# A hybrid layer on one core: no barrier between batches, and another order of the first projections and value tiles

## The chip, the cores and the metric

One Trainium2 chip, one of its cores. The metric is the device time of one execution in microseconds (us). The core's engines work side by side, each through its own list of instructions in order, and meet at semaphores: TensorE (PE: matrix products and transposes, into PSUM), VectorE (DVE), ScalarE (ACT), GpSimd (POOL), and SyncE (SP), which issues most DMA transfers. PSUM has eight banks of 128 x 512 float32.

## The reference

Four batches of 1024 tokens, 512 wide, go through four sublayers. Each has a layer norm in front and is added to its input:

```python
x = x + attention(layernorm(x))   # 16 heads of 32, Wqkv 512 x 1536; softmax over keys, Wo
x = x + experts(layernorm(x))     # 8 experts of rank 16, the best 2 by softmax gates
x = x + ssm(layernorm(x))         # 32 heads, state 64, depthwise convolution, gated, W_out
x = x + experts(layernorm(x))     # the same experts again
```

In the attention, `kqv = x @ Wqkv + bqkv` is cut in three; the scores are of k against q under a triangular mask, a softmax over the keys weighs v. Nothing of one batch enters another.

## The kernel before, in words

A loop on every engine runs over the batches (b, 0 to 3). A float32 product at full precision is made as three products of float32r halves ("hi" and "lo"; `three`, L713 to L717): ScalarE rounds a tile to its hi part, VectorE or GpSimd subtracts for the lo part.

**Layer norm.** Token tiles t = 0 to 7 of 128 tokens. VectorE takes statistics (`tile_stats`, L1345), GpSimd the inverse root in two halves of four tiles (`inverse_roots`, L1747), VectorE normalises a tile into `xh` (`center`, L1371), TensorE transposes it in four pieces (`turn`, L725), ScalarE copies the hi part into `uh` (L1126), VectorE makes the lo part `ul` (`lo`, L1362). `by_tile` puts a product of tile t-1 behind the transposes of tile t. `add_tiles` adds a stage's result to X and, where another layer norm follows, takes the statistics of tile t-1 between additions and normalises the first two tiles at t = 5.

**Opening of the attention.** A value tile is 12 matmuls, one token tile times the value weights wv (`values`), evicted by VectorE with its bias (`value`, L1471). A projection of a head group (4 heads) is four pieces: ch 0 and 1 are the first operand for tokens 0 to 511 and 512 to 1023, ch 2 and 3 the second; 12 matmuls each (`project`), evicted by ScalarE (hi, L1179) and VectorE (lo, L1488). Then DMAs (`stack`, L461) bring the parts of each pair of heads into rows QS and KS. A first pass of scores (`scores_a`, L830, 16 steps t16) is only for each row's maximum, which VectorE takes (L1496); the maxima are turned (L838), copied and sent by DMA into QS as one more row. The second pass (`scores_b`, L850) makes scores with the maximum subtracted; ScalarE takes exponentials (L1202), TensorE weighs the values (L867, L869). While one pair of heads is weighed, the first pass of the next pair and the next group's projection run between its steps.

Before, value tiles 0 to 3 lie among the transposes, then come tiles 4 to 7's transposes without products, the four projection pieces of group 0, and value tiles 4 and 5, 6, and 7 ahead of score steps 0, 4 and 8 (`EARLY`, `BETWEEN`).

**Group weights.** The weights of a head group go to `win` in two steps: a cast on ScalarE (`group_hi`, L1149) and a subtraction on GpSimd (`group_lo`, L1751, one instruction). The value weights take four casts (L1165) and four subtractions. On GpSimd, the second half of the inverse roots, the copies of the values (VG, L1773), a memset and eight additions of the bias bo to X (L1785) stand in the opening; then comes group_lo of the next group.

**Batch boundary.** The last expert stage ends with additions to X. `barrier` then holds TensorE, ScalarE, VectorE and GpSimd until all have come; SyncE stores the tiles of X as they are done, and loads the next batch's tokens into X, a tile behind its store (L534). The weights of the value product and of head group 0 are loaded beside the expert stage, after the row product of the ssm stage.

## Time and profile before

| | |
|---|---|
| median of 3 runs | 3359.28 us (3359.22 to 3366.12) |
| the profiled execution's own time | 3359.53 us |
| its span in the profile | 3357.7 us |
| TensorE busy | 3056.9 us, 91% of the span |
| VectorE busy | 2206.4 us, 66% |
| ScalarE busy | 1095.1 us, 33% |
| GpSimd busy | 753.4 us, 22% |
| mean granted clock of TensorE | 0.94 |

The span is from the first to the last instruction. "Granted clock" (PEclk) is the share of full speed that the chip gives TensorE: it is 1.0 (2.4 GHz) or 0.5 (1.2 GHz), and a stretch between is a mixture. The program's start lasts until about 113 us, then come four batches of some 812 us. A row of the timeline has its start, its length, the engine, the kernel's line, the operation, its output <- its inputs and how many instructions it sums up; in brackets the engine's idle time before it and what ended it. Matmuls overlap, so that the length of one is more than the step from one to the next.

### The profile page before, as it was taken

The page shows a single profiled execution, that of the slowest core. Times are in us where ns is not written, and L with a number is a line of the kernel's source. Part 1 is how long each engine was busy: PE and PEld are TensorE (multiplying, and loading weights), DVE is VectorE, ACT ScalarE, POOL GpSimd, SP SyncE. Part 2 cuts the span into 40 slices and gives each one's busy share as a digit, 9 for nine tenths or more (in the row PEclk, how much of TensorE's full clock was granted, in tenths as well). Part 3 has the DMA queues.
Part 4 walks back from the last instruction along what each step waited for, and adds up shares of the span by engine and source line. Part 5 has one row for each costly group of instructions (what it writes and reads, how often), then busy time and mean ns, then how long its engine had stood idle before and what let it go on. Part 6 is the DMA issues. An engine that isn't in the chain of part 4 may idle for free.

```text
span 3357.7 us, 59614 instructions
## 1 busy us (share of the span) xinstructions
PE 3056.9 (91%) x20772; PEld 2086.8 (62%) x20772; DVE 2206.4 (66%) x2961; ACT 1095.1 (33%) x1728; POOL 753.4 (22%) x1065
## 2 busy tenths in 40 slices
PE   3599999999879998999978999999997999999998
PEld 3445457777555446777755444777775454577775
DVE  1356667777646667777764666777764566677776
ACT  1123314444113333344312332343421233143441
POOL 3121102333031111233311110133321211013331
PEclk6789999999979999999988999999998899999999
DMA  7422102111131211111121220111112121021111
GB/s 228 149 50 63 45 13 64 51 48 44 49 82 44 63 26 46 50 48 44 35 83 45 63 63 20 51 44 51 42 43 83 45 69 45 13 63 50 48 42 51
DMA packets 160037, 189.47 MB, mean 56 GB/s; under 512 B 43834, under 2 KB 103866, under 8 KB 158074
## 3 DMA queue, kind: packets, MB, share of 16 engines
q1 hardware_dynamic: 155998, 173.74, 18.8%
q0 software_dynamic: 2720, 10.49, 0.8%
q10 hardware_dynamic: 1152, 3.15, 0.4%
q8 instruction: 89, 1.46, 0.2%
q14 instruction: 78, 0.64, 0.1%
HBM read 104.90 MB, written 23.36 MB: 38 GB/s over the span
## 4 chain that ended last, share of the span: by engine, by line
PE 77%; DVE 9%; issue 4%; DMA 4%; SPq 3%; ACT 2%; POOL 1%; DVEq 0%; POOLq 0%; ACTq 0%
PE ps L715 13%; PE ps L717 12%; PE ps L716 12%; PE ps L867 7%; PE ps L830 5%; PE ps L850 5%; PE ps L1026 4%; PE ps L912 3%; PE ps L1012 2%; DVE mneg L1496 2%; PE ps L760 2%; PE ps L1072 2%; DVE LM L1590 2%; PE ps L1035 2%; PE ps L725 1%
## 5 line engine op out<-in xcount | busy, mean ns | idle before, releaser
L715 PE MATMUL ps<-uh,win 128*128 128x512 f32 x1536 | 631.1, 411 | 10.5 <-DVE ul L1362 5.9
L717 PE MATMUL ps<-uh,win 128*128 128x512 f32 x1536 | 606.0, 395 | 0.0
L716 PE MATMUL ps<-ul,win 128*128 128x512 f32 x1536 | 602.9, 393 | 0.0
L1496 DVE TENSOR_REDUCE mneg<-ps 128x1 f32<-128x128 f32 (+7 forms) x512 | 360.5, 751 | 164.6 <-PE ps L833 160.9
L1202 ACT ACTIVATE PR<-ps 128x1024 f32<-128x1024 f32 (+3 forms) x384 | 310.6, 810 | 430.1 <-PE ps L853 292.8
L867 PE MATMUL ps<-PR,VG 128*32 128x512 f32 (+3 forms) x1536 | 346.3, 528 | 10.8 <-DVE OS L1502 8.3
L715 PEld LDWEIGHTS ps<-uh,win 128*128 128x128 f32 x1536 | 291.5, 190 | 103.7 <-issue 36.5
L869 PE MATMUL ps<-PR,ones 128*32 128x512 f32 (+3 forms) x1536 | 346.3, 528 | 0.0
L717 PEld LDWEIGHTS ps<-uh,win 128*128 128x128 f32 x1536 | 290.6, 189 | 65.9
L1614 DVE TENSOR_TENSOR LM<-ps,LM 128x512 f32<-128x512 f32 x256 | 170.2, 686 | 241.5 <-PE ps L1026 197.1
L716 PEld LDWEIGHTS ps<-ul,win 128*128 128x128 f32 x1536 | 291.9, 190 | 55.1
L1838 POOL TENSOR_SCALAR_AFFINE_SELECT LM<-LM 128x512 f32<-128x512 f32 x256 | 209.0, 827 | 490.8 <-ACT LM L1281 490.8
L850 PE MATMUL ps<-QS,KS 97*128 97x512 f32 (+3 forms) x768 | 274.6, 424 | 15.5 <-DMA QS<-mrow 8.9
L830 PE MATMUL ps<-KS,QS 96*128 96x512 f32 (+3 forms) x768 | 247.2, 422 | 26.6 <-DMA KS<-EV 16.4
L1801 POOL TENSOR_TENSOR OT<-OS,rec 64x512 f32 (+1 forms) x64 | 82.5, 1288 | 838.5 <-DVE rec L1509 838.5
L1602 DVE SCALAR_TENSOR_TENSOR Ct<-ps,cpt,Ct 128x1023 f32<-128x1023 f32 (+2 forms) x192 | 245.5, 1279 | 16.6 <-ACT Ct L1271 12.1
L1602 DVE SCALAR_TENSOR_TENSOR Bt<-ps,cpt,Bt 128x1023 f32<-128x1023 f32 (+2 forms) x192 | 243.5, 1268 | 0.3
L850 PEld LDWEIGHTS ps<-QS,KS 97*128 97x128 f32 x768 | 148.1, 207 | 137.8 <-issue 90.8
L830 PEld LDWEIGHTS ps<-KS,QS 96*128 96x128 f32 x768 | 139.4, 211 | 137.4 <-DVE mneg L1496 70.1
L1126 ACT CAST uh<-ps 128x512 fp32r<-128x512 f32 x128 | 74.0, 588 | 453.0 <-PE ps L725 453.0
L1509 DVE RECIPROCAL rec<-OS 64x256 f32<-64x256 f32 (+1 forms) x96 | 214.6, 2261 | 2.1
L1281 ACT ACTIVATE LM<-ps 128x512 f32<-128x512 f32 x256 | 147.6, 602 | 124.3 <-PE ps L1012 124.1
(218 smaller groups left out, 5149.6 us busy)
## 6 DMA issues: line engine op xcount, KB each, us to landing
raw<-in_t SPq DMA_DIRECT2D x128, 256.0 KB, 2.8
QS<-EV SPq DMA_DIRECT2D x192, 128.0 KB, 2.4
KS<-EV SPq DMA_DIRECT2D x168, 128.0 KB, 2.4
X<-in_L_attn_b_W_in_dram SPq DMA_DIRECT2D x10, 1024.0 KB, 8.0
in_t<-tiles POOLq DMA_DIRECT2D x10, 1024.0 KB, 9.0
win_raw<-in_L_attn_a_Wqkv_dram SPq DMA_DIRECT2D x34, 256.0 KB, 3.5
X<-in_L_attn_a_x_dram SPq DMA_DIRECT2D x32, 256.0 KB, 3.9
win_raw<-in_t SPq DMA_DIRECT2D x32, 256.0 KB, 2.7
```

The lines of the kernel that those rows point to most:

```text
L715: pe.matmul(dst, hi_l, hi_r, start=first, stop=False)
L716: pe.matmul(dst, hi_l, lo_r, start=False, stop=False)
L717: return pe.matmul(dst, lo_l, hi_r, start=False, stop=last)
L830: i = pe.matmul(ps[:, b0 + c // HB, 0:m], QS[slot][0:STACK, hh, t * P:(t + 1) * P], KS[slot][0:STACK, hh, c:c + m], start=True, stop=not diag)
L850: i = pe.matmul(ps[:, SCORE_BANK[u] + hh, 0:n], KS[slot][:, hh, s * P:(s + 1) * P], QS[slot][:, hh, t0:t0 + n], start=True, stop=not diag)
L867: pe.matmul(ps[o:o + HS, 6, at:at + n], VG[:, s, h:h + HS], PR[:, u % 2, hh, 0:n], start=(s == 0), stop=last)
L869: i = pe.matmul(ps[r:r + HS, 6, at:at + n], ones[:, 0:HS], PR[:, u % 2, hh, 0:n], start=(s == 0), stop=last)
L1202: act.activation(PR[:, u % 2, :, 0:n], ps[:, SCORE_BANK[u]:SCORE_BANK[u] + 2, 0:n], ACT.Exp, scale=SCALE).then_inc(ex.sem, 1)
L1496: dve.tensor_reduce(mneg[:, hh, t:t + 1], wide(b0)[:, 0:(t + 1) * P], AX.X, ALU.max, negate=True).then_inc(a_max.sem, 1)
L1509: i = dve.reciprocal(rec[hf * 64:(hf + 1) * 64, cols], OS[(1 - hf) * 64:(2 - hf) * 64, cols])
L1602: dve.scalar_tensor_tensor(dst[:, par, k:L], wide(2 * w)[:, 0:L - k], cpt[:, par, w, at:at + 1], dst[:, par, k:L], ALU.mult, ALU.add).then ...
L1838: pool.affine_select(out=v, in_=v, compare_op=ALU.is_ge, fill=0.0, base=0, pattern=[[0, 4], [1, P]], channel_multiplier=-1).then_inc(sel_p ...
```

## The change

1. The barrier is gone. The tokens of the next batch are loaded into a tile XN of their own (in memory that OT and other tiles use at other times), right behind the row product of the ssm stage, ahead of the last expert stage's stores. Statistics and the first two normalised tiles of the next batch are taken in `add_tiles` of the last expert stage. The bias addition on GpSimd becomes X = XN + bob.
2. The value weights of the next batch are loaded at the last pair of the ssm stage, cast and subtracted at that stage's end (`value_hi`, `value_lo`). Group 0's cast (`group_hi`) follows the first exponentials of the last expert stage on ScalarE; its subtraction and the first half of the inverse roots follow on GpSimd. For batch 0 all this stands ahead of the loop.
3. The opening has another order: transposes 0 and 1, value tile 0, transposes 2, value tile 1, transposes 3 to 5, the projection piece ch 0, transposes 6, ch 2, transposes 7, value tile 2, ch 1, ch 3, value tiles 3 and 4; tiles 5 and 6 in quarters (`value_part`) between score steps, tile 7 half ahead of the turned maxima and half behind them.
4. The row tiles of the second slot lie over wv now, so SyncE waits for the last value tile before it fills them. In the last batch the prepared "next" batch is batch 3 again, and nothing uses it.

```diff
-EARLY = HALF
-BETWEEN = {0: (4, 5), 4: (6,), 8: (7,)}
+FIRST_OF = (0, 2, 1, 3)
+BETWEEN = {3: (5, 0), 5: (5, 1), 6: (5, 2), 7: (5, 3), 11: (6, 0), 13: (6, 1), 14: (6, 2), 15: (6, 3)}
+def value_bank(t):
+    return 2 + t % 2 if t < 4 else t
+def first_at(ch):
+    return FIRST_OF.index(ch) + 1
...
-        def barrier(eng, b):
-            eng.sem_inc(s_tick, 1)
-            eng.drain().then_inc(s_bar, 1)
-            eng.wait_ge(s_bar, b * 5 + 10)
-            eng.sem_inc(s_tick, 1)
...
+                XN = sb("XN", [P, TT, D], at=c2)
...
 SyncE
-                    sp.wait_ge(s_out[t], b * 16 + 16)
-                    sp.dma_start(X[:, t, :], x[bass.ds(b, 1), t * P:(t + 1) * P, :].rearrange("a p d -> p (a d)")).then_inc(s_x[t], 16)
+                    sp.dma_start(XN[:, t, :], x[bass.ds(b, 1), t * P:(t + 1) * P, :].rearrange("a p d -> p (a d)")).then_inc(s_x[t], 16)
...
+                            v_pe.wait(sp, b, TT)
                             st_pe.wait(sp, b * 8 + g * 2, 0)
                             stack(sp, 1)
...
+                                if last and q == 3:
+                                    xp_pool.wait(sp, b * PAIRS + j, 1)
+                                    value_weights()
                                 save_y(j, q)
...
                     w_pe.wait(sp, b * 2 + 1, TT)
-                first_weights()
-                sp.sem_inc(s_tick, 1)
-                sp.drain().then_inc(s_bar, 1)
+                    group_weights(0)
+                    load_tokens(b if end else b + 1)
...
 TensorE
+                turn(b * 4, 0)
+                turn(b * 4, 1)
+                values(0)
+                turn(b * 4, 2)
+                values(1)
+                for t in range(3, 6):
+                    turn(b * 4, t)
+                ln_lo.wait(pe, b * 4, 4)
+                project(0, 0, True)
+                turn(b * 4, 6)
+                project(0, 2, True)
+                turn(b * 4, 7)
+                values(2)
                 ln_lo.wait(pe, b * 4, TT)
-                for ch in range(4):
-                    project(0, ch, True)
+                project(0, 1, True)
+                project(0, 3, True)
+                values(3)
+                values(4)
+                v_done.wait(pe, b, 4)
                 for t16 in range(16):
-                    late_values(t16)
+                    if t16 in BETWEEN:
+                        value_part(*BETWEEN[t16])
                     scores_a(b * 8, 0, b * 4, t16)
+                for k in range(2):
+                    value_part(7, k)
                 turn_maxima(b * 8)
+                for k in range(2, KT):
+                    value_part(7, k)
                 pe.wait_ge(s_kone, b * 2 + 1)
-                v_done.wait(pe, b, TT)
                 scores_b(b * 8, 0, b * 4, 0)
+                v_done.wait(pe, b, TT)
...
 ScalarE
-                experts(b * 4 + 3, b * 2 + 1)
-                barrier(act, b)
+                value_hi(b + 1)
+                experts(b * 4 + 3, b * 2 + 1, lambda: group_hi(b * 4 + 4))
...
 VectorE
+                def behind(t):
+                    if t < 2:
+                        value(t)
+                    elif t == 4:
+                        project_lo(0, 0, True)
+                    elif t == 5:
+                        project_lo(0, 2, True)
+                    elif t == 6:
+                        value(2)
+                by_tile(b * 4, behind, lambda: loaded(b, TT - 1), XN)
...
-                experts(b * 4 + 3, b * 2 + 1, None, lambda: w_add.wait(dve, b * 2 + 1, TT))
-                barrier(dve, b)
+                experts(b * 4 + 3, b * 2 + 1, b * 4 + 4, lambda: w_add.wait(dve, b * 2 + 1, TT), XN, lambda t: loaded(b + 1, t))
...
 GpSimd
+            value_lo(0)
+            inverse_roots(0, (0,))
+            group_lo(0)
+            with pool.Fori(0, NB) as b:
+                inverse_roots(b * 4, (1,))
...
-                    i = pool.tensor_tensor(X[:, t, :], X[:, t, :], bob[:, :], ALU.add)
+                    pool.wait_ge(s_out[t], b * 16 + 16)
+                    pool.sem_inc(s_tick, 1)
+                    i = pool.tensor_tensor(X[:, t, :], XN[:, t, :], bob[:, :], ALU.add)
...
+                value_lo(b + 1)
                 inverse_roots(b * 4 + 3)
-                barrier(pool, b)
+                group_lo(b * 4 + 4)
+                inverse_roots(b * 4 + 4, (0,))
```

TensorE behind the last product of a value tile among the transposes (xh the normalised tile, win the group's weights), before:

```order
L717 MATMUL ps<-wv,ul 128x512
L95 REGISTER_ALU
L725 MATMUL ps<-ident,xh 128x128 x4
L95 REGISTER_ALU
L725 MATMUL ps<-ident,xh 128x128 x4
L95 REGISTER_ALU
L725 MATMUL ps<-ident,xh 128x128 x4
L95 REGISTER_ALU
L715 MATMUL ps<-uh,win 128x512
```

and in the changed kernel:

```order
L725 MATMUL ps<-wv,ul 128x512
L103 REGISTER_ALU
L733 MATMUL ps<-ident,xh 128x128 x4
L103 REGISTER_ALU
L733 MATMUL ps<-ident,xh 128x128 x4
L103 REGISTER_ALU
L733 MATMUL ps<-ident,xh 128x128 x4
L103 REGISTER_ALU
L723 MATMUL ps<-uh,win 128x512
```

The rows read alike, but before they are tiles 5, 6 and 7 behind value tile 3, and now tiles 3, 4 and 5 behind value tile 1, so that the first projection piece has two more tiles' transposes still to come.

TensorE between the first pass of scores (its mask's matmul is the first row) and the second, with the transpose of the maxima mneg, before:

```order
L833 MATMUL ps<-mask_ts,identb 128x128
L95 REGISTER_ALU
L838 MATMUL ps<-ident,mneg 16x128
L880 ISA
L95 REGISTER_ALU
L844 ISA
L95 REGISTER_ALU
L850 MATMUL ps<-QS,KS 128x512
```

and in the changed kernel, up to the waits ahead of the second pass:

```order
L725 MATMUL ps<-wv,ul 128x512
L103 REGISTER_ALU
L846 MATMUL ps<-ident,mneg 16x128
L723 MATMUL ps<-wv,uh 128x512
L724 MATMUL ps<-wv,uh 128x512
L725 MATMUL ps<-wv,ul 128x512
L723 MATMUL ps<-wv,uh 128x512
L724 MATMUL ps<-wv,uh 128x512
L725 MATMUL ps<-wv,ul 128x512
L909 ISA
L852 ISA
```

Half of value tile 7 stands ahead of the transpose of the maxima, and the other half behind it.

GpSimd at the end of a batch, behind the last selection in the ssm stage, before:

```order
L1838 AFFINE_SELECT LM<-LM 128x512
L95 ISA
L1747 TENSOR_TENSOR rstd<-veps,halfs 128x4
L95 REGISTER_ALU
L1747 TENSOR_TENSOR rstd<-veps,halfs 128x4
L346 ISA
```

and in the changed kernel, from the last two subtractions for wv on:

```order
L1796 TENSOR_TENSOR wv<-wv_raw,wv 128x512
L103 REGISTER_ALU
L1796 TENSOR_TENSOR wv<-wv_raw,wv 128x512
L103 ISA
L1792 TENSOR_TENSOR rstd<-veps,halfs 128x4
L103 REGISTER_ALU
L1792 TENSOR_TENSOR rstd<-veps,halfs 128x4
L103 REGISTER_ALU
L1796 TENSOR_TENSOR win<-win_raw,win 128x2x512
L103 ISA
L1792 TENSOR_TENSOR rstd<-veps,halfs 128x4
```

In place of the barrier's signal stand the next batch's group_lo and the first half of its inverse roots, and ahead of the stage's own roots the value weights.

## Rows read from the trace of the kernel before

**Rows 1.** The page, part 1: busy us, share of the span, instructions.

```profile
PE 3056.9 (91%) x20772; PEld 2086.8 (62%) x20772; DVE 2206.4 (66%) x2961; ACT 1095.1 (33%) x1728; POOL 753.4 (22%) x1065
```

**Rows 2.** Waits: engine, line, for whom; us in total, times, longest.

```profile
PE ps L725 <- DVE xh L1371: 68.9, 12, 18.7
```

**Rows 3.** Timeline, TensorE: first transposes of batches 1, 2 and 3.

```profile
932.14 1.97 PE L725 MATMUL ps<-ident,xh 128*128 128x128 f32 x8 [14.96 <-DVE xh L1371]
...
1744.88 1.54 PE L725 MATMUL ps<-ident,xh 128*128 128x128 f32 x6 [15.29 <-DVE xh L1371]
...
2557.45 1.97 PE L725 MATMUL ps<-ident,xh 128*128 128x128 f32 x8 [15.18 <-DVE xh L1371]
```

**Rows 4.** Timeline, batch 1's opening: TensorE, and VectorE's last eight maxima.

```profile
954.70 0.79 PE L715 MATMUL ps<-uh,win 128*128 128x512 f32 x1 [1.48 <-DVE ul L1362]
...
972.79 0.22 PE L830 MATMUL ps<-KS,QS 96*128 96x128 f32 x1
...
983.51 5.54 DVE L1496 TENSOR_REDUCE mneg<-ps 128x1 f32<-128x128 f32 x8
...
989.11 0.38 PE L838 MATMUL ps<-ident,mneg 128*16 128x128 f32 x1 [1.32 <-DVE mneg L1496]
991.71 0.79 PE L850 MATMUL ps<-QS,KS 97*128 97x512 f32 x1 [2.22 <-DMA QS<-mrow]
```

**Rows 5.** Timeline, TensorE: the opening of batch 0, first and last.

```profile
122.78 1.54 PE L725 MATMUL ps<-ident,xh 128*128 128x128 f32 x6 [18.66 <-DVE xh L1371]
...
179.46 0.79 PE L850 MATMUL ps<-QS,KS 97*128 97x512 f32 x1 [2.22 <-DMA QS<-mrow]
```

**Rows 6.** Windows: stretch, its us, busy by engine (instructions), PEclk, DMA share, GB/s.

```profile
957.00:970.00 13.00, 13.00 (x57) 10.64 (x56) 3.01 (x4) 2.75 (x4) 0.00 (x0) 0.97 0.27 62
...
897.00:907.00 10.00, 6.32 (x15) 2.22 (x13) 8.72 (x38) 1.26 (x7) 0.00 (x0) 0.66 0.00 1
490.30:493.70 3.40, 3.40 (x19) 3.40 (x18) 2.84 (x10) 0.23 (x1) 2.31 (x2) 0.50 0.01 2
991.70:1009.10 17.40, 16.90 (x76) 7.94 (x76) 4.44 (x7) 5.16 (x7) 7.57 (x6) 0.50 0.51 122
```

**Rows 7.** Timeline, TensorE: first expert stage of batch 0 into the next norm.

```profile
486.89 0.49 PE L761 MATMUL ps<-bu,w3T 24*128 24x512 f32 x1
487.31 1.09 PE L725 MATMUL ps<-ident,xh 128*128 128x128 f32 x8
489.92 0.39 PE L715 MATMUL ps<-waw,uh 128*128 128x256 f32 x1 [1.51 <-DVE ul L1362]
```

**Rows 8.** Timeline: GpSimd and VectorE together; the gates' exponentials; TensorE behind the gates.

```profile
492.49 2.70 POOL L1751 TENSOR_TENSOR win<-win_raw,win 128x512 fp32r<-128x512 f32 x2
492.73 1.31 DVE L1371 TENSOR_SCALAR xh<-X,mv,rstd 128x512 f32<-128x512 f32 x1
...
895.87 0.23 ACT L1133 ACTIVATE gex<-ge_ 128x32 f32<-128x32 f32 x1 [1.07 <-DVE ge_ L1416]
...
900.86 0.47 PE L753 MATMUL ps<-ident,hg 128*128 128x128 f32 x1 [3.60 <-DVE hg L1436]
```

**Rows 9.** Timeline, GpSimd: from the value copies to the next group's subtraction.

```profile
983.76 1.16 POOL L1773 COPY VG<-V 128x512 f32<-128x512 f32 x2 [33.78 <-DVE V L1471]
...
987.06 9.85 POOL L1785 TENSOR_TENSOR X<-X,bob 128x512 f32<-128x512 f32 x8 [0.18 <-POOL KS L1781]
997.33 2.36 POOL L1751 TENSOR_TENSOR win<-win_raw,win 128x1024 fp32r<-128x1024 f32 x1 [0.42 <-POOL X L1785]
```

**Rows 10.** Timeline, ScalarE: first and seventh exponentials of two pairs of heads.

```profile
993.33 1.30 ACT L1202 ACTIVATE PR<-ps 128x1024 f32<-128x1024 f32 x2 [3.55 <-PE ps L853]
...
1014.24 0.59 ACT L1202 ACTIVATE PR<-ps 128x512 f32<-128x512 f32 x1
...
313.25 1.02 ACT L1202 ACTIVATE PR<-ps 128x1024 f32<-128x1024 f32 x1 [0.83 <-PE ps L853]
...
328.23 0.59 ACT L1202 ACTIVATE PR<-ps 128x512 f32<-128x512 f32 x1
```

More of the change, by code:

```diff
@@ L726, in turn, with by_tile @@
                 i.then_inc(ln_tp.sem, 1)
-            def by_tile(n, product, tiles=TT):
+            def by_tile(n, product):
                 for t in range(TT + 1):
@@ L1120, in _, with turn @@
             first_barrier(act)
-            def turn(n):
-                for t in range(TT):
+            def turn(n, tiles=range(TT)):
+                for t in tiles:
                     ln_tp.wait(act, n, t + 1)
@@ L1176, in project_hi @@
                                 act.wait_ge(s_stack[i][hh], (b * 4 + g) * 96)
-                    pj.wait(act, b * 4 + g, ch + 1)
+                    pj.wait(act, b * 4 + g, first_at(ch) if first else ch + 1)
                     act.sem_inc(s_tick, 1)
@@ L1395, in add_tiles, with experts @@
                     dve.tensor_tensor(X[:, t, :], ps[:, bank + t % 4, :], X[:, t, :], ALU.add).then_inc(added.sem, 1)
[L1396 to L1398 removed]
+                    if t >= 1:
+                        if loaded is None:
+                            added.wait(dve, n, t)
+                        else:
+                            loaded(t - 1)
+                        tile_stats(stats_of, t - 1, src)
                         if t == HALF + 1:
[L1400 to L1402 removed]
+                            first_tiles(stats_of, src)
+            def experts(n, f, stats_of, last_added, src=X, loaded=None):
                 ch = Chain(dve, s_gates, 26, f)
@@ L1456, in pair_lo, with loaded @@
                                   ALU.subtract).then_inc(bcw_lo.sem, 1)
+            def loaded(b, t):
+                dve.wait_ge(s_x[t], b * 16 + 16)
+                dve.sem_inc(s_tick, 1)
+            for t in range(TT - 1):
+                loaded(0, t)
+                tile_stats(0, t, XN)
+                if t == HALF:
+                    first_tiles(0, XN)
             with dve.Fori(0, NB) as b:
@@ L1486, in project_lo @@
                     cols = slice(c * HB, (c + 1) * HB)
-                    pj_hi.wait(dve, b * 4 + g, ch + 1)
+                    pj_hi.wait(dve, b * 4 + g, first_at(ch) if first else ch + 1)
                     dve.scalar_tensor_tensor(EV[w][1][:, cols], ps[:, 4 + ch if first else 7, :],
@@ L1490, in project_lo @@
                                              EV[w][0][:, cols].bitcast(F32), ALU.add, ALU.subtract).then_inc(pj_lo.sem, 1)
+                def behind(t):
[8 more added lines that the diff above has]
+                by_tile(b * 4, behind, lambda: loaded(b, TT - 1), XN)
+                project_lo(0, 1, True)
+                project_lo(0, 3, True)
+                for t in range(3, 5):
+                    value(t)
                 def maximum(p, t16):
@@ L1740, in until, with inverse_roots @@
                 pool.sem_inc(s_tick, 1)
-            def inverse_roots(n):
-                for h in range(2):
+            def inverse_roots(n, halves=(0, 1)):
+                for h in halves:
                     until(ln_var, n, h + 1)
```

371 lines of the change are left out of this document (183 added, 188 removed).

## The prediction

> **What bounds the kernel now.** I read the page first: TensorE is busy for 91% of the span [rows 1], so only two things can move the end by much: time in which TensorE stands still, and time in which it runs at the lower clock. The waits come next: TensorE's costliest wait is for the first transposes of a layer norm, 68.9 us in 12 waits [rows 2]. The timeline says where: the three largest inside the loop stand at the batch boundaries, 14.96, 15.29 and 15.18 us [rows 3]. All engines meet at the barrier there, the tokens are loaded, their statistics taken, and only then does TensorE start. Last I read the opening of the attention stage, piece by piece, in a batch behind a boundary [rows 4] and in the first [rows 5], and the granted clock of a few stretches [rows 6].
>
> The opening runs from the first transpose (932.14) to the first score matmul of the second pass (991.71): 59.6 us [rows 3, 4]. At the full clock a matmul of this kind takes 13.0/57 = 0.228 us [rows 6], so a value tile or a projection (12 matmuls) is 2.74 us. The 12 of them are 32.8 us; the rest is scores, transposes, standing still and low clock. In the first batch it takes 179.46 - 122.78 = 56.7 us [rows 5].
>
> **The change part by part.**
>
> *A. Boundary.* The barrier goes; tokens land in a tile of their own, XN, issued before the second expert stage, and VectorE takes their statistics and first two normalised tiles between its last additions. This trace has a stage built so already, the first expert stage into the next layer norm: the last expert matmul starts at 486.89, the transposes at 487.31, with no idle time between them [rows 7]. I take that for all three boundaries: 14.96 + 15.29 + 15.18 = **45.4 us off**. Were the tokens late, part of the stand would stay, so the bounds are 0 and 45.4; but the load is issued ahead of the whole expert stage and read behind its end, so I take all of it. What is late next is the chain from transpose to the first product, 489.92 - 487.31 = 2.6 us [rows 7].
>
> *B. Opening.* From the first transpose on: 2.6 us to the first product [rows 7]; then, before the first score, five value tiles and four projections, 108 x 0.228 = 24.6; six more groups of transposes at 0.4 us (half of some 0.8 for eight in [rows 7]) 2.4; a stretch at the low clock like the 3.4 us behind the same kind of start [rows 6], which costs half of it, 1.7; one gap while transposes 3 to 5 follow each other without a product between them. Before, tiles 5 to 7 stood so, and their last wait alone was 1.48 [rows 4]; I take 1.6, and 0.9 for a one-in-two chance that the clock falls there again. Sum 33.8. Then the scores: VectorE's maxima for one half take 5.54 us [rows 4], two halves 11.1, and and I estimate one value copy at 0.7, the start at 0.3 and waits for free banks at 1.7: 13.8 until the last maximum. TensorE's own work there, two value tiles in quarters (5.5) and scores (an estimated 6), is less and lies beside it; half of the last value tile follows while the last maxima run. Then 0.5 to the transpose of the maxima and its 991.71 - 989.11 = 2.6 us to the second pass [rows 4], which now hides the other half tile. Total 33.8 + 13.8 + 0.5 + 2.6 = 50.7 against 59.6: 8.9 each in three batches, **26.6 off**. Bounds: nothing in the opening runs faster than work plus the two chains (about 46), and 59.6 is what it takes now.
>
> *C. First batch.* There GpSimd's subtraction for the first head group (group_lo) now comes right behind the first half of the inverse roots, that is beside VectorE's first two normalisations. The nearest row of such a meeting: GpSimd started at 492.49, VectorE's normalisation, begun at 492.73, ended at 494.04, just behind the end of GpSimd's first instruction (2.70/2 = 1.35 us, to 493.84) [rows 8]. Group_lo is one instruction of 2.36 us [rows 9], so the bounds are 0 and 2.4 and I take 2.4 lost; a little low clock that the old opening had there too gives 1.2 less than in B. 50.7 + 2.4 - 1.2 = 51.9 against 56.7: **4.8 off**.
>
> *D. The first pair of heads.* Behind the opening TensorE ran at the low clock for the whole of 991.7 to 1009.1, busy for 16.9 of 17.4 us [rows 6]. From the first exponential to the seventh it took 1014.24 - 993.33 = 20.9 us; the same piece of a later group took 328.23 - 313.25 = 15.0 [rows 10]. So a full clock would be worth 5.9 us a batch. It can't be had whole: GpSimd is queued behind the last value tile with two copies, a memset, eight additions of 9.85 us and group_lo, 999.69 - 983.76 = 15.9 us [rows 9], and these now start some 0.3 us behind the first score matmul of the second pass, where they started 8 us ahead of it. The next projection needs group_lo; with its 2.74 us and 1.1 more to the seventh exponential that one can't come before 20.0 us, against 22.5 now (1014.24 - 991.71). So 0 to 2.5 a batch; I take 1.3, **5.2 off**.
>
> *E. Expert stage.* ScalarE casts the next batch's group weights right behind the first exponentials (895.87 [rows 8]), so GpSimd's group_lo of 2.36 us starts near 897.3, in the middle of VectorE's chain of small gate operations, which ends what TensorE waits for: it stood still for 3.60 us until 900.86 [rows 8]. If VectorE is held as it was at 492.73, the chain is late by what is left of 2.36. Bounds 0 and 2.4; I take 2.4, since the chain is a row of short operations with gaps into which the long one can fall: 4 x 2.4 = **9.6 lost**. The longer stand also keeps the clock low for longer than the few us of 897 to 907 (0.66 granted [rows 6]): 0 to 4 a batch, taken as 1, **4 lost**. The Trainium skill (SBUF — State Buffer, "SBUF: two separate sides") says that a VectorE operation with two inputs in SBUF is blocked for the whole of a GpSimd operation that reads SBUF; most gate operations are of that kind. The row at 492.73 is of another kind and agrees as far as it goes; without that rule I would have put E at half.
>
> *F. Costed at nothing.* The value weights are loaded, cast and subtracted behind the last pair's mixing, while VectorE's last gate and TensorE's row product run: ScalarE and GpSimd have nothing else there. If GpSimd's four subtractions (4 x 9.85/8 = 4.9 us by [rows 9]) came 2 us late they would meet VectorE's last gate, up to 5 us. The additions of the bias now read XN; their wait for the stores of the last batch was over long before. SyncE's wait for the last value tile ahead of the second slot's rows is over before it gets there; behind it stand only those row copies. The reload of tokens after the last batch is hidden by the expert stage.
>
> **Sum.** 45.4 + 26.6 + 4.8 + 5.2 - 9.6 - 4 = 68.4 us off. The profiled execution took 3359.5 us (span 3357.7), 0.2 above the median of 3359.28, so no correction: 3359.5 - 68.4 = **3291 us**.
>
> **Rivals.**
> *1. The clock holds and the gates aren't held up.* E goes (13.6), the 0.9 and 1.7 of B mostly go (some 8 in all): 3269. For: 957 to 970 ran at 0.97 [rows 6]. Against: each start behind a stand of 1.5 us or more in these rows has a low stretch behind it. 0.20.
> *2. Low clock for long.* In one of the two places (behind the gates, behind transposes 3 to 5) the clock stays low for some 20 us as in 991.7 to 1009.1 [rows 6], not 3.4: (20 - 3.4)/2 = 8.3 a batch, 3291 + 33 = 3324. For: the stand behind the gates grows from 3.6 to 6 us. 0.16.
> *3. The stretch doesn't do what it says:* the overlap works, but the reordered opening is paced by VectorE and ScalarE, whose in-order queues now carry a projection's halves between tiles (ul, EV, V one behind the other), and gives nothing, or the boundary keeps a third of its stand for a late load: 3291 + 31 = 3322 at the middle, 3307 to 3337. Against: each tile has 2.74 us of products beside it, and VectorE has an estimated 2 us of work a tile. 0.12.
> *4. Slower than before.* The low clock takes the opening and the pairs behind it: at half speed every 2 us of busy time lose 1. It decides from 68.4/4 = 17 us lost a batch, that is 34 us more of TensorE's time at the low level than now; with 50 us more a batch it is 25 x 4 = 100 lost, 3391. For: 17.4 us in one piece stand there now. Against: the change takes stands away everywhere but behind the gates. 0.04.
> The forecast has 0.48, within 3277 to 3307.
>
> **Range and chances.** 3291 is the likeliest. The range takes in rival 1 and rivals 2 and 3 to their middles: 3265 to 3324; left out are rival 4, the far half of 3, and the tails. A measurement of this kernel tells 0.2% (7 us) from no change. Faster is all but rival 4 and a remnant for mishaps: 0.95; same 0.01; slower 0.04.
>
> **What would show it.** A: no wait of TensorE near 15 us at the three boundaries, transposes within 0.5 us of the last expert matmul. B: first transpose to first score of the second pass in 49 to 53 us; if over 56, the reordering failed. D: first to seventh exponential under 19 us, and a wait of the next projection for GpSimd's subtraction. E: a gate operation of VectorE that takes over 2 us, and TensorE's wait behind the gates at 6 us instead of 3.6. I am wrong if the first-to-last times of an expert stage don't grow (then E), or if a stretch of 20 us at the low clock stands in a new place (rival 2).

## The result, and the profile after

The changed kernel takes **3305.8 us** (median of 4 runs, 3297.8 to 3327.7) against 3359.6 beside it: ratio **0.984, 95% interval 0.981 to 0.988**. A second comparison gave 0.985 (0.981 to 0.989). The forecast of 3291 us (3265 to 3324) holds: faster, by 54 us where 68 were worked out. The profiled execution took 3303.4 us, so I read 56 us out of its trace. Ratios and ranges, here and below, are of fast runs; left out as slow are one run of the second comparison (10760.6 us) and two of experiment 5 (3397.6 and 3398.6).

| | before | after |
|---|---|---|
| profiled execution / span, us | 3359.5 / 3357.7 | 3303.4 / 3301.8 |
| mean granted clock | 0.94 | 0.952 |
| TensorE busy, us | [rows 1] | 3038.8 |

The page, part 1:

```profile
PE 3038.8 (92%) x20772; PEld 2076.8 (63%) x20772; DVE 2220.3 (67%) x2975; ACT 1095.8 (33%) x1733; POOL 759.9 (23%) x1071
```

Waits (engine, line, for whom: us in total, times, longest), against [rows 2]:

```profile
PE ps L761 <- DVE hg L1475: 37.5, 8, 5.8
PE ps L733 <- DVE xh L1407: 25.5, 9, 20.7
PE ps L838 <- DMA KS<-EV: 21.6, 19, 1.4
PE ps L723 <- POOL win L1796: 8.9, 6, 3.3
```

The wait for the first transposes fell from 68.9 to 25.5 us; what is left is mostly the 20.7 of the very first, before batch 0. The wait for the gated tiles (hg) has grown from 28.9 us to 37.5, and that for GpSimd's subtraction (win) from 4.0 to 8.9.

**A, boundary.** TensorE at the first boundary, and VectorE beside it, against [rows 3]:

```profile
914.80 0.50 PE L769 MATMUL ps<-bu,w3T 24*128 24x512 f32 x1
916.81 1.16 PE L733 MATMUL ps<-ident,xh 128*128 128x128 f32 x8 [1.51 <-issue]
```

```profile
916.50 0.68 DVE L1381 BATCH_NORM_STATS2 stats<-XN 128x6 f32<-128x512 f32 x1
918.67 0.69 DVE L1398 TENSOR_TENSOR ul<-ps,uh 128x512 fp32r<-128x512 f32 x1 [1.50 <-ACT uh L1155]
```

From the last expert matmul to the next transposes it takes 2.01, 2.02 and 2.47 us, before 15.45, 15.79 and 15.67 (starts, the idle time of [rows 3] and the last matmul's own time): 40.4 us off. The stand that is left is put down to "issue": TensorE waited for no other engine.

**B, C, opening.** First scores and second pass of batch 1, and a window behind the boundary (stretch, its us, busy by engine, PEclk, DMA share, GB/s), against [rows 4, 6]:

```profile
952.12 0.33 PE L838 MATMUL ps<-KS,QS 96*128 96x128 f32 x1 [0.84 <-DMA KS<-EV]
...
969.09 0.49 PE L858 MATMUL ps<-QS,KS 97*128 97x512 f32 x1 [0.82 <-DMA QS<-mrow]
```

```profile
917.70:924.50 6.80, 5.27 (x14) 3.95 (x13) 2.89 (x9) 0.89 (x2) 2.94 (x2) 0.50 0.56 184
```

969.09 - 916.81 = 52.3 us, in the other two batches 51.7 and 51.8, before 59.6, 59.3 and 59.2: 22.2 off. In batch 0 the opening is 51.7 against 56.7, 4.9 off. The meeting foreseen in C took place, ahead of the first transposes; the row of the same two normalisations before, and three rows now:

```profile
122.18 1.00 DVE L1371 TENSOR_SCALAR xh<-X,mv,rstd 128x512 f32<-128x512 f32 x2 [0.61 <-POOL rstd L1747]
```

```profile
119.85 2.33 POOL L1796 TENSOR_TENSOR win<-win_raw,win 128x1024 fp32r<-128x1024 f32 x1
119.90 3.03 DVE L1407 TENSOR_SCALAR xh<-XN,mv,rstd 128x512 f32<-128x512 f32 x2 [0.59 <-POOL rstd L1792]
122.52 1.12 PE L733 MATMUL ps<-ident,xh 128*128 128x128 f32 x4 [20.66 <-DVE xh L1407]
```

**D, first pair of heads.** First and seventh exponential, and the next projection on TensorE, against [rows 9, 10]:

```profile
970.05 1.30 ACT L1238 ACTIVATE PR<-ps 128x1024 f32<-128x1024 f32 x2 [2.89 <-PE ps L861]
...
990.76 0.59 ACT L1238 ACTIVATE PR<-ps 128x512 f32<-128x512 f32 x1
```

```profile
985.36 0.50 PE L723 MATMUL ps<-uh,win 128*128 128x512 f32 x1 [3.28 <-POOL win L1796]
```

The window from the first exponential until the subtraction is done, and the one from there to the seventh exponential:

```profile
970.00:985.30 15.30, 10.12 (x79) 4.94 (x77) 6.24 (x9) 5.00 (x7) 14.38 (x11) 1.00 0.57 133
985.30:990.80 5.50, 5.44 (x25) 4.09 (x25) 0.00 (x0) 0.62 (x2) 0.00 (x1) 0.69 0.00 0
```

From the second pass to the seventh exponential it is 21.2 to 21.7 us, before 22.4 to 22.5: 4.2 off in four batches.

**E, second expert stage.** GpSimd and VectorE, then TensorE behind the gates, the stage's first transposes ahead of them, and the window behind, against [rows 6, 8]:

```profile
873.92 1.04 PE L733 MATMUL ps<-ident,xh 128*128 128x128 f32 x8
...
891.05 2.34 POOL L1796 TENSOR_TENSOR win<-win_raw,win 128x1024 fp32r<-128x1024 f32 x1 [12.39 <-ACT win L1180]
891.09 2.58 DVE L1462 SCALAR_TENSOR_TENSOR gq<-gt,before 128x256 f32<-128x256 f32 x1
893.71 0.42 DVE L1463 SCALAR_TENSOR_TENSOR gq<-gt,gq 128x256 f32<-128x256 f32 x1
...
896.86 0.48 PE L761 MATMUL ps<-ident,hg 128*128 128x128 f32 x1 [5.76 <-DVE hg L1475]
```

```profile
893.80:907.50 13.70, 10.56 (x20) 3.98 (x21) 10.24 (x39) 1.67 (x9) 0.00 (x0) 0.50 0.11 39
```

The gate operation gq takes 2.58 us, beside GpSimd's subtraction of 2.34, where the like one behind it takes 0.42. TensorE stands for 5.76 instead of 3.60 us, and the clock is at its lower level for all of 893.8 to 907.5 (before, 897 to 907 had a mean of 0.66). From the first transposes to the last matmul, 914.80 - 873.92 = 40.9 us, in the others 39.7, 41.0 and 40.9; before 36.3 to 36.6: 16.4 lost. Of these 8.6 lie in the first half of the stage, up to the transposes of the gated tiles, with 2.15 in every batch (22.95 us against 20.80); 7.8 lie in the second half, and that part varies: 17.9, 16.7, 18.1 and 17.9 us in this trace, 14.6, 14.8, 19.5 and 16.6 in the second trace of the same kernel, before 15.5 to 15.8.

Sum: 40.4 + 22.2 + 4.9 + 4.2 - 16.4 = 55.3 of the spans' 55.9. The stages that the sum leaves out moved too, and nearly cancel: the attention behind the first pair is 4.7 us shorter in sum, the ssm stage 2.7 longer and the first expert stage 1.0.

### The profile page after: what moved, and what is told of

It is laid out like the page before. It is cut to its first block, busy times and chain, and to the rows that moved or that the text cites. A ratio compares the mean times of both kernels' runs of the same rounds, so it can differ in the third digit from the quotient of the medians.

```text
span 3301.8 us, 59660 instructions
## 1 busy us (share of the span) xinstructions
PE 3038.8 (92%) x20772; PEld 2076.8 (63%) x20772; DVE 2220.3 (67%) x2975; ACT 1095.8 (33%) x1733; POOL 759.9 (23%) x1071
## 4 chain that ended last, share of the span: by engine, by line
PE 76%; DVE 9%; issue 4%; DMA 4%; SPq 3%; ACT 2%; POOL 1%; ACTq 0%; DVEq 0%; POOLq 0%
PE ps L723 13%; PE ps L725 12%; PE ps L724 12%; PE ps L875 7%; PE ps L838 5%; PE ps L858 5%; PE ps L1056 4%; PE ps L942 3%; PE ps L1042 2%; PE ps L1102 2%; DVE LM L1636 2%; PE ps L1065 2%; PE ps L768 2%; DMA KS<-EV 1%; DVE mneg L1543 1%
## 5 line engine op out<-in xcount | busy, mean ns | idle before, releaser
L875 PE MATMUL ps<-PR,VG 128*32 128x512 f32 (+3 forms) x1536 | 338.3, 517 | 12.4 <-DVE OS L1549 8.3
L877 PE MATMUL ps<-PR,ones 128*32 128x512 f32 (+3 forms) x1536 | 338.3, 517 | 0.0
L858 PE MATMUL ps<-QS,KS 97*128 97x512 f32 (+3 forms) x768 | 266.4, 414 | 9.9 <-ACT PR L1238 6.6
L838 PE MATMUL ps<-KS,QS 96*128 96x512 f32 (+3 forms) x768 | 239.4, 411 | 29.1 <-DMA KS<-EV 21.6
L1648 DVE SCALAR_TENSOR_TENSOR Ct<-ps,cpt,Ct 128x1023 f32<-128x1023 f32 (+2 forms) x192 | 245.6, 1279 | 16.6 <-ACT Ct L1307 12.0
```

What stands on the lines that cost most here:

```text
L838: i = pe.matmul(ps[:, b0 + c // HB, 0:m], QS[slot][0:STACK, hh, t * P:(t + 1) * P], KS[slot][0:STACK, hh, c:c + m], start=True, stop=not diag)
L858: i = pe.matmul(ps[:, SCORE_BANK[u] + hh, 0:n], KS[slot][:, hh, s * P:(s + 1) * P], QS[slot][:, hh, t0:t0 + n], start=True, stop=not diag)
L875: pe.matmul(ps[o:o + HS, 6, at:at + n], VG[:, s, h:h + HS], PR[:, u % 2, hh, 0:n], start=(s == 0), stop=last)
L877: i = pe.matmul(ps[r:r + HS, 6, at:at + n], ones[:, 0:HS], PR[:, u % 2, hh, 0:n], start=(s == 0), stop=last)
L1648: dve.scalar_tensor_tensor(dst[:, par, k:L], wide(2 * w)[:, 0:L - k], cpt[:, par, w, at:at + 1], dst[:, par, k:L], ALU.mult, ALU.add).then ...
```

## The experiments

Each ratio is to the kernel before, timed beside the variant. The changed kernel and the late cast were timed beside each other once, in the second comparison.

**1. The late cast** (timed three times, the second and third beside other variants).

```diff
                 exponentials(0)
-                if meanwhile is not None:
-                    meanwhile()
@@ (loop over t, behind the copies of a tile)
+                    if t == 4 and meanwhile is not None:
+                        meanwhile()
```

> The changed kernel, but ScalarE casts the next batch's group weights behind the fifth pair of copies of the last expert stage, not behind the first exponentials; GpSimd's subtraction follows it there, behind VectorE's gate operations. Theory (GpSimd's subtraction of 2.34 us holds VectorE's gate operation for as long as it runs): no gate operation over 0.5 us, TensorE's longest wait behind the gates back from 5.8 to about 3.6 us, second expert stage from its first transposes to its last matmul back from 40.6 to 36.6-37.5 us in each batch, 13 to 16 us off the changed kernel's 3303.4: 3288 to 3291. Rival 1 (the stage is longer because VectorE now does the next batch's statistics between its additions, or because the clock falls there anyway): it stays at 40 us or more, the time within 3 us of 3303. Rival 2 (the block only moves, to VectorE's additions or the first normalised tiles): the gates are free, but the last additions or the next first transposes come up to 2.3 us later, and of the 13 us under 6 are left.

Measured: 3275.2 us, ratio **0.976** (0.973 to 0.979).

```profile
PE ps L761 <- DVE hg L1475: 28.8, 8, 3.6
```

```profile
886.45 0.42 DVE L1462 SCALAR_TENSOR_TENSOR gq<-gt,before 128x256 f32<-128x256 f32 x1
...
890.07 0.47 PE L761 MATMUL ps<-ident,hg 128*128 128x128 f32 x1 [3.61 <-DVE hg L1475]
```

The operation is back at 0.42 us, the stage at 36.3, 35.8, 35.4 and 36.4 us: 18.6 us less than with the early cast. So rival 1 falls. The boundaries got 1.7 us longer in sum, but only 0.2 in the second pair of traces, so rival 2 isn't shown. The spans differ by 29.9 us. The other 13 lie in stages that the edit doesn't touch: the attention stages behind the first pair are 9.3 us shorter, at a mean granted clock of 0.962 instead of 0.952 over the whole run.

> The changed kernel itself once more, beside its variants on one chip. Both theories expect the 0.984 of the first comparison (3306), within 3295 to 3320, since the granted clock differs from run to run.

> The kernel of the late cast once more, beside the changed kernel on the same chip. Its first comparison gave 3275 where 16 us off 3304 were expected from the stage alone. Theory A (the stand behind the gates also set how long the clock stays low behind it, in the expert stage and in the stages that follow): the distance to the changed kernel stays 25 us or more, with a mean granted clock higher by about 0.01. Theory B (the surplus was chance of one profiled run and four timings): 14 to 20 us off the changed kernel.

Measured on one chip: 0.985 (0.981 to 0.989) for the changed kernel, 0.976 (0.973 to 0.980) for the late cast. That is 28 us apart, near theory A, but by these intervals uncertain by some 18 us, so that the 14 to 20 of theory B aren't excluded; and the granted clock, averaged over the runs, is higher by 0.004 (0.951 and 0.956), not by theory A's 0.01. A third time the late cast gave 0.979 (0.975 to 0.983), as expected there:

> The late cast once more, as the yardstick for the next kernel on the same chip: 0.976 of the kernel before, within 0.973 to 0.980.

What the traces show in every pair is the hold: the first half of the stage takes 22.95 us with the early cast and 20.80 with the late one, 8.6 us in four batches. The rest goes with the clock. The whole stage took 162.4 and 157.3 us (four batches) in the two traces of the changed kernel, and 143.8, 151.0 and 158.5 in the three of the late cast; two batches of the third took 43.0 us, each with 20 us at the low clock behind the usual stand of 3.6. The times put the edit at some 24 to 28 us, give or take 10 to 18. That this is more than the hold of 8.6 is likely by the times; by which path a shorter stand would give a higher clock these runs don't show, and no single trace carries it (in the second comparison the two profiled runs were at 0.955 and 0.957).

**2. Memsets in place of the subtraction** (the low part of the next head group's weights is zero in batches 1 to 3).

```diff
-                group_lo(b * 4 + 4)
+                until(qkw_hi, b * 4 + 4, 1)
+                pool.memset(win[:, 0, 0, 1].bitcast(F32), 0.0)
+                pool.memset(win[:, 0, 1, 1].bitcast(F32), 0.0).then_inc(qkw_lo.sem, 1)
```

> The changed kernel, but in the last expert stage of each batch GpSimd fills the low part of the next head group's weights with zeros in two memsets, at the place where it subtracted (so this low part is left out of the computation in batches 1 to 3; GpSimd writes as many elements to the same tile, and reads none). Theory (it is the read of two tiles in SBUF by GpSimd that holds VectorE's operation with two inputs in SBUF): the gate operation gq takes 0.43 us beside the memsets, the stage 36.6-37.5 us. Rival (any work of GpSimd at that time holds VectorE, or the write alone): gq takes as long as the memsets that it meets, 1 us or more, the stage 39 us or more.

```profile
885.30 0.52 POOL L1921 MEMSET win<- 128x512 f32 x1 [12.39 <-ACT win L1180]
885.36 0.42 DVE L1462 SCALAR_TENSOR_TENSOR gq<-gt,before 128x256 f32<-128x256 f32 x1
885.77 0.52 POOL L1922 MEMSET win<- 128x512 f32 x1
888.97 0.48 PE L761 MATMUL ps<-ident,hg 128*128 128x128 f32 x1 [3.60 <-DVE hg L1475]
```

One run, 3280.0 us. The gate operation ran its 0.42 us wholly inside the first memset, at the same place. Theory right: what held it was that GpSimd read SBUF. That a memset is shorter isn't the reason: experiment 3's subtractions are as short (3.70/8 = 0.46 us) and still hold it. This is the rule that the prediction took from the Trainium skill (SBUF — State Buffer, "SBUF: two separate sides"), both of its halves now shown: a GpSimd operation that reads held gq, one that only writes didn't. Three of the four stages took 36.3 to 36.7 us; that of batch 0 took 43.0, with 20 us at the low clock behind the usual 3.6 us stand. So the clock behind the same stand varies.

**3. The subtraction in eight.**

```diff
-                group_lo(b * 4 + 4)
+                until(qkw_hi, b * 4 + 4, 1)
+                for w in range(2):
+                    for k in range(KT):
+                        i = lo_in_place(win[:, 0, w, 0, k], win[:, 0, w, 1, k], win_raw[:, 0, w, 1, k])
+                i.then_inc(qkw_lo.sem, 1)
```

> The changed kernel with the early cast, but in the last expert stage GpSimd's subtraction of 128x1024 goes as eight of 128x128. Theory (VectorE is held for as long as the one GpSimd instruction that it meets runs, so short ones hold it for a part each, and each further gate operation with two inputs in SBUF for the next part): gq takes under 1 us, but the whole chain of gate operations is late by 1 us or more, the stage's first half ends 0.8 to 2.2 us later than in the kernel before. Rival (VectorE goes first between two short instructions and is no longer held): from the stage's first transposes to the first transposes of gated tiles 21.0 us or less.

```profile
889.09 3.70 POOL L1796 TENSOR_TENSOR win<-win_raw,win 128x128 fp32r<-128x128 f32 x8 [12.41 <-ACT win L1180]
889.13 0.70 DVE L1462 SCALAR_TENSOR_TENSOR gq<-gt,before 128x256 f32<-128x256 f32 x1
889.86 0.56 DVE L1463 SCALAR_TENSOR_TENSOR gq<-gt,gq 128x256 f32<-128x256 f32 x1
```

gq took 0.70, the first half of the stage 21.98 us in every batch: 1.18 late, where one piece made it 2.15 and none 0 (20.80). Theory right. Small pieces halve the hold (one run, 3286.1 us), but putting the subtraction elsewhere takes it away.

**4. The boundary alone**: the changed kernel with the old opening.

```diff
-FIRST_OF = (0, 2, 1, 3)
-BETWEEN = {3: (5, 0), 5: (5, 1), 6: (5, 2), 7: (5, 3), 11: (6, 0), ...}
+FIRST_OF = (0, 1, 2, 3)
+BETWEEN = {0: (4, 5), 4: (6,), 8: (7,)}
...
+                for t in range(TT + 1):
+                    if t < TT:
+                        turn(b * 4, t)
+                    if t >= 1:
+                        ln_lo.wait(pe, b * 4, t)
+                        if t <= HALF:
+                            for k in range(KT):
+                                value_part(t - 1, k)
+                for ch in range(4):
+                    project(0, ch, True)
```

> The changed kernel with the old order in the opening of the attention stage (four value tiles among the transposes, four projections, four value tiles between the scores), but no barrier and the next batch prepared early. Theory (the parts add up): boundaries 40 us shorter than before, second expert stages 16 us longer in sum, opening 59 us as before, first batch and first pair unchanged: 3359.5 - 40 + 16 = 3335, within 3330 to 3341. Rival (the two parts need each other: the early preparation puts the stand into the opening unless the transposes are followed by products at once): openings of batches 1 to 3 above 61 us, time 3342 or more. Rival 2 (the loss in the expert stage comes with the new opening, not with the overlap): expert stage at 36.6, time about 3319.

Measured: 3328.8 us, ratio 0.991 (0.988 to 0.994), 1 us under the expected range. Boundaries 2.2 to 2.8 us, second expert stages 37.6 to 39.7, openings 57.2, 57.3, 56.7 and 56.4. In batches 1 to 3 the openings are 2 to 3 us shorter than before without any new order, which no theory had. The trace has the reason: up to the first score TensorE was at the low clock for 12.1, 11.7 and 11.5 us before, with 8.1 to 8.7 of them right behind the stand of 15 us; behind a stand of 2 to 3 us it is 6.8, 3.4 and 3.4. The overlap alone is worth some 30 us, and the new order on top of it 0.991 - 0.984 = 0.7%, 23 us.

**5. The new order alone**: the kernel before with the new opening, barrier and loading as they were. The functions are those of the change; only VectorE's list differs, since the last two statistics are still taken among the tiles:

```diff
+                def behind(t):
+                    if t < 2:
+                        loaded_stats(t + 6)
+                        value(t)
```

> The kernel before with only the new order in the opening (the first head group projected by halves among the transposes, value tiles 5 to 7 in parts between and behind the scores); barrier and loading at the start of a batch as before. Theory (the parts add up): opening 52 instead of 59.6 us in batches 1 to 3 and 52 instead of 56.7 in batch 0, first pair about 1 us shorter each, boundaries 15.5 us and expert stages 36.6 us as before: 22 + 5 + 4 = 31 us off, 3328, within 3322 to 3334. Rival (the new order depends on the statistics being done ahead; with two of VectorE's statistics among the tiles and GpSimd's subtraction behind both inverse roots the products wait for them): opening 56 us or more, time 3342 or more.

Measured: 3360.9 us (median of eight runs), ratio **0.998** (0.995 to 1.002), scattered from 3330 to 3375. Theory wrong, the rival nearer, though two openings are under its 56 us. The opening of batch 0 (GpSimd, VectorE, TensorE):

```profile
132.63 1.98 DVE L1406 TENSOR_SCALAR xh<-X,mv,rstd 128x512 f32<-128x512 f32 x1
134.48 1.87 POOL L1809 MEMSET KS<- 1x2048 f32 x1 [0.16 <-POOL win L1793]
...
134.66 1.12 PE L734 MATMUL ps<-ident,xh 128*128 128x128 f32 x4 [1.83 <-DVE xh L1406]
135.13 1.50 DVE L1406 TENSOR_SCALAR xh<-X,mv,rstd 128x512 f32<-128x512 f32 x1
```

Without the early preparation the second half of the inverse roots and the subtraction (131.81 to 134.33) come among the tiles. Normalisations that take 0.55 us take 1.98 and 1.50, and TensorE waits 1.29 and 1.83 us for them. The openings take 56.5, 54.7, 56.3 and 53.3 us: 13.9 off instead of the 27 with both parts. And the attention stages behind the first pair are 18.3 us longer than before; the granted clock of this run is 0.938. Whether the new order brings this on is open: the same stages, 1013 us in sum here, lie between 981 and 1009 in the other traces, and this profiled run is 8 us slower than the median. The parts don't add up: experiment 4's 30 us and this one's 6 (uncertain by 11) make 36 of the 54. In the openings the trace says why: the new order pays fully only with the statistics and the subtraction out of its way.

**6. The bias later** (on top of the late cast). GpSimd's batch loop's first group is unrolled, and the eight additions stand behind its subtraction:

```diff
-                for t in range(TT):
-                    ...
-                    i = pool.tensor_tensor(X[:, t, :], XN[:, t, :], bob[:, :], ALU.add)
...
                                 until(qkw_lo, b * 4 + g + 1, 1)
+                                if stage == 0:
+                                    for t in range(TT):
+                                        ...
+                                        i = pool.tensor_tensor(X[:, t, :], XN[:, t, :], bob[:, :], ALU.add)
```

> The late cast, and GpSimd's eight additions of the bias moved behind its subtraction for the second head group. Theory (this order is what makes TensorE wait 3.28 us for the subtraction in the first pair of heads): this wait is gone, from the first to the seventh exponential 17 to 18.5 instead of 20.5 us, 8 to 12 us off the kernel with the late cast alone in four batches. Rival (the low clock behind the opening sets this piece, and only fills the time that the wait took, or the earlier work brings the low clock back): the piece stays above 20 us, under 3 us off.

Measured: 0.978 (0.974 to 0.982), the late cast alone on that chip 0.976: no gain seen, though the theory's 8 to 12 us lie within these intervals. The granted clock, averaged over the runs, is 0.951 against 0.956. Two windows, of batches 1 and 3:

```profile
983.00:1004.00 21.00, 20.19 (x108) 10.69 (x106) 6.94 (x10) 6.27 (x9) 14.36 (x11) 0.67 0.41 96
2566.00:2584.00 18.00, 16.04 (x120) 9.37 (x123) 7.96 (x14) 6.26 (x10) 14.82 (x12) 1.00 0.47 115
```

TensorE's wait of 3.28 us is gone in all batches, yet the seven exponentials take 23.6, 20.4, 20.5 and 15.7 us: only where the clock was full (1.00) did the piece come near its 15 us. In the others it was at the lower level for 20.5, 13.7 and 13.7 us; the window of 983 to 1004, behind the opening of batch 1, has TensorE busy for 20.19 of 21 us at 0.67. So the rival holds in three of four batches. With the next edit on top, two of four batches took 15.4 and 15.6 us; in the traces with the additions at their old place none took under 19.

**7. The branch early**, on top of 6 and then without it.

```diff
+            turn(0, 0)
+            turn(0, 1)
             with pe.Fori(0, NB) as b:
-                turn(b * 4, 0)
-                turn(b * 4, 1)
                 ...
                 experts(b * 4 + 3, b * 2 + 1)
+                turn(b * 4 + 4, 0)
+                turn(b * 4 + 4, 1)
@@ vector, before the loop with b = 0 and at its end with b + 1
+                lo(b * 4, 0)
+                loaded(b, TT - 1)
+                tile_stats(b * 4, TT - 1, XN)
```

> The kernel before this one, and the batch loop's end moved: TensorE issues the next batch's first two tiles of transposes, and VectorE the first low half and the last statistics, ahead of the branch back to the loop's start instead of behind it. Theory (the 2.0 to 2.9 us between the last expert matmul and the next transposes are TensorE's branch of 3.5 us, and the first product waits for VectorE's branch too): transposes within 0.6 us of the last matmul, from the last expert matmul to the first product 3.0 to 3.6 instead of 4.7 us, 3 to 5 us off in three boundaries. Rival (the branch only moves to the next place where an engine is waited for): the last matmul to the third tile of transposes takes as long as now, within 1 us of the kernel before this one.

> The late cast, and the batch loop's end moved behind the next batch's first transposes, with GpSimd's bias additions back at their old place. Theory (the branch is hidden and what the kernel with all three edits lost came from the bias additions, behind which the clock fell): 3 to 5 us off the late cast alone, mean granted clock as there. Rival (each stand of TensorE that goes is paid for by a longer stretch at the low clock, wherever the stand was): granted clock lower by 0.004 or more, time the same as the late cast's or up to 12 us more.

```profile
913.29 0.49 PE L769 MATMUL ps<-bu,w3T 24*128 24x512 f32 x1
913.72 1.09 PE L733 MATMUL ps<-ident,xh 128*128 128x128 f32 x8
917.62 0.49 PE L723 MATMUL ps<-wv,uh 128*128 128x512 f32 x1 [2.81 <-issue]
```

These rows are of the first kernel. The transposes follow the last matmul by 0.42 us, as first predicted for the change, so the 2 us were the branch. But it now stands ahead of the first product: last matmul to first product 4.3, 3.8 and 4.2 us here, 4.7 to 5.1 in the changed kernel and 4.9 to 5.5 with the late cast. To the third tile of transposes it is 8.5 and 8.1 us in two boundaries (10.0 to 10.3 with the late cast) and 10.5 in the third, at the low clock. So the first kernel's theory is right on the transposes and missed its 3.0 to 3.6 us for the product; its rival's "within 1 us" holds in one boundary of three. The times show no gain: 0.982 (0.978 to 0.986) with experiment 6's edit, 0.981 (0.979 to 0.984) without, the late cast on that second chip 0.979 (0.975 to 0.983). An edit of 3 to 5 us is finer than these intervals. The second kernel's rival has the time right; its clock, in the mean 0.951 against the late cast's 0.954, fell by 0.003 where 0.004 or more was asked, within the scatter of single runs (0.947 to 0.960).

**Nothing was clearly faster than the changed kernel with the late cast**: 0.976, 0.976 and 0.979, some 2.3% under the kernel before.

## Why the prediction was right, and where it was 13 us off

| term | predicted | measured in the trace |
|---|---|---|
| A boundary | 45.4 off | 40.4 off |
| B opening, batches 1 to 3 | 26.6 off | 22.2 off |
| C first batch | 4.8 off | 4.9 off, by luck |
| D first pair | 5.2 off | 4.2 off |
| E expert stage | 13.6 lost | 16.4 lost |

**A** was mis-sized by its model. The first expert stage runs into the next norm in straight code; the second ends a batch, and behind it TensorE branches back to the loop's start. The trace's record of this branch lasts 3.5 us (913.13 to 916.63), partly beside matmuls already issued. Before, it ran from 918.25 to 922.12, while TensorE stood for VectorE until 932.14 anyway: it was hidden. Experiment 7 shows that the 2 us are the branch's. I had asked whether the load or the transposes' chain would be late; nothing was late but the instructions themselves.

**B** is off by 1.2 us a batch, and by 0.7 because I took batch 1's 59.6 for all three. The clock is low for 6.8 us behind the boundary's stand, not 3.4; that is 1.7 us by the prediction's own price. TensorE waits 0.84 us for the copies into KS ahead of the first score, for which I had no term. Against that the clock didn't fall in the gap among the transposes (0.9). The second pass starts 14.5 + 2.5 us behind the first score, as worked out (14.3 + 2.6). What the 8.9 a batch didn't name is that a part of them belongs to A: the stand of 15 us left the clock low for over 8 us of the old opening, and experiment 4 has 2 to 3 us of the gain without any new order.

**C** came out by luck. The hold took place: the two normalisations beside GpSimd's subtraction took 3.03 us instead of 1.00. But it lies ahead of the first transposes, which come 2.6 us behind the start of the normalisations instead of 0.6. These 2.0 us are outside the interval that was summed, and the earlier statistics covered them (first transposes at 122.52, before 122.78). Inside it batch 0 took 51.7 us like the other batches, and not 1.2 more than they. The prediction had added those 1.2 to a B that was 1.2 too short.

**D** held in its mechanism, and one term of it was mis-sized. TensorE waited 3.28 us for GpSimd. The subtraction ended 16.2 us behind the second pass, as worked out (0.3 + 15.9); from there to the seventh exponential it took 5.0 to 5.5 us, where 2.74 + 1.1 stood. The windows show why: the clock was full until the wait, and fell behind it, so that the 12 matmuls of the projection took 4.4 us (985.36 to 989.80). Over the four batches the piece had between 3.4 and 13.7 us at the low clock, before 17.3, and yet took 21.2 to 21.7 us in each: while GpSimd's queue is in the way, less low clock ahead of it brings nothing. My criterion "under 19 us from first to seventh exponential" didn't fit my own figure: 22.5 - 1.3 = 21.2 counted from the second pass is 19.6 from the first exponential. The trace has 20.2 to 20.7. Experiment 6 adds that with the queue out of the way the low clock limits the piece.

**E** came as predicted: the meeting, the operation over 2 us, the stand of about 6. The hold itself cost 2.15 us a batch, 8.6 of 9.6 predicted. The stage's second half lost 7.8 instead of 4 in this trace, but 2.7 in the second trace of the same kernel, and the late cast's third trace, without the hold, lost 12.5 there. So of E's two terms the hold is shown, and the one for a longer low clock can't be put down to the longer stand. Experiments 1 to 3 show the hold from three sides. Its price in the whole run may be higher than its stage shows (experiment 1).

**F** came as costed: GpSimd's four subtractions for the value weights ran from 848.09 for 4.97 us and were over before VectorE's last gate began at 854.82.

Of the rivals, the first (no hold, the clock holds) is near to what the late cast brought: it was given 3269, and the three timings have 3275, 3284 and 3292, without a full clock. The long low stretch of rival 2 didn't show in the changed kernel, but did in single batches of its variants. Rival 3's slow opening appeared only without the overlap (experiment 5), where work of GpSimd among the tiles held VectorE. The 8.9 us a batch of B were therefore right only in company with A, which the prediction didn't say. And its "0.2% from no change" was too fine: the interval of the comparison is 0.4% to either side.

## What to carry to other kernels

Before putting GpSimd work that reads SBUF into a stage that another engine waits for, list VectorE's operations there: here one with two inputs in SBUF waited for the whole GpSimd instruction (2.58 us instead of 0.42). Move the GpSimd work by a few microseconds rather than cut it up. When a barrier goes, look for the branch at the loop's end in its place. Check that a cost lies inside the interval that you sum: C's did not. And don't count on small waits of a TensorE that is busy for nine tenths of the time: of three waits of 2 to 3 us that the experiments shortened, moved or took away, only the one behind the gates shortened the run by more than the times' scatter. One trace isn't enough to price the clock: the same stage with the same stand took 35.4 to 43.0 us.

## What the runs showed of the hardware

- The branch at the end of the batch loop, one pass of which is some 14,700 recorded instructions over all engines, lasts 3.3 to 5.4 us in TensorE's records of all traces; no branch of the inner loops lasted over 0.25 us. VectorE's own record of that branch is short (0.06 us), but its next record begins 2.85 us behind it (915.55 to 918.40). Why the branch takes so long the traces don't show.
- A GpSimd memset on one partition held a normalisation of VectorE (a tensor_scalar with one tile as input in SBUF), 1.50 instead of 0.55 us (experiment 5), while a memset on 128 partitions left the operation with two inputs alone (experiment 2). The same page and section of the Trainium skill names both: an operation in a mode that uses both of VectorE's ports is held by any GpSimd operation, one with two inputs only by a GpSimd operation that reads. That the normalisation ran in such a mode no trace shows; the two times fit it.
- With the same instructions the first pair of heads took 15.7 us to its seventh exponential with no time at the low clock, and 23.6 us with 20.5 us of it (experiment 6). The runs of one kernel on one chip spread over 0.5 to 1.3%, so edits of 0.1 to 0.2% could be read only from the trace.
